# A two-layer gated cross-attention kernel: maxima subtracted on VectorE, three transposed low parts on GpSimd, all instruction streams in a new order

## The reference

```
x = x + tanh(g) * attention0(norm(x), ctx)    # 16 heads; softmax over the heads, not over the keys
x = x + tanh(g) * ffn0(norm(x))               # silu(x Wg) * (x Wu), hidden size 768, then Wd
x = x + tanh(g) * attention1(norm(x), ctx)    # 16 query heads, one shared key and value head
x = x + tanh(g) * ffn1(norm(x))               # one 256x256 matrix: W plus a low-rank product, and a bias
norm(x) = (x - mean(x)) / sqrt(var(x) + 1e-5)
```

## Time and profile before

| | |
|---|---|
| median of 3 runs | 2554.6 us (2552.17 to 2556.8) |
| the profiled execution | 2554.42 us |
| its span, first to last instruction | 2552.6 us |
| mean granted TensorE clock | 0.996 of full speed |
| busy: PE, DVE, ACT, POOL | 2463.6, 2311.4, 1616.7, 1476.5 us |

### The profile page before, as it was taken

The page is one execution under the profiler, slowest core; times in us unless marked ns, Lnnn a source line. Parts: engine busy times, 40 slices in busy tenths (PEclk is TensorE's granted clock), DMA queues, the critical chain, the costliest instruction groups (busy, mean ns, idle before and its releaser), DMA issues.

```text
span 2552.6 us, 70067 instructions
## 1 busy us (share of the span) xinstructions
PE 2463.6 (97%) x27972; PEld 2151.3 (84%) x27972; DVE 2311.4 (91%) x4254; ACT 1616.7 (63%) x3210; POOL 1476.5 (58%) x1806
## 2 busy tenths in 40 slices
PE   6999999999999999999999999999999999999997
PEld 5888888888888888888888888888888888888886
DVE  7889999999999999999999999999999999999974
ACT  4466666666666666666666666666666666666653
POOL 3555565565565565665665665665665665655642
PEclk9999999999999999999999999999999999999999
DMA  3000010010000010010110110110110100110100
GB/s 101 20 28 25 25 33 22 28 33 21 29 31 23 29 31 23 29 31 19 33 31 19 33 31 19 33 31 19 33 31 19 33 31 19 33 31 19 30 18 14
DMA packets 74322, 73.20 MB, mean 29 GB/s; under 512 B 6555, under 2 KB 73393, under 8 KB 74290
## 3 DMA queue, kind: packets, MB, share of 16 engines
q1 hardware_dynamic: 74290, 72.75, 9.2%
HBM read 54.90 MB, written 16.78 MB: 28 GB/s over the span
## 4 chain that ended last, share of the span: by engine, by line
PE 48%; DVE 46%; issue 3%; ACT 1%; POOL 0%; DMA 0%; SPq 0%; POOLq 0%; DVEq 0%; ACTq 0%
PE work L1849 11%; PE work L1850 9%; PE work L1851 9%; DVE m L1284 6%; DVE e L1302 6%; DVE m L1293 5%; PE scores L1952 5%; PE work L1985 5%; DVE x L1321 4%; DVE y_q L1312 3%; PE scores L1942 3%; DVE scores L1290 3%; PE work L1888 3%; PE work L1866 2%; DVE work L1298 2%
## 5 line engine op out<-in xcount | busy, mean ns | idle before, releaser
L731 ACT ACTIVATE e<-scores 120x1024 f32<-120x1024 f32 x512 | 497.4, 1023 | 133.2 <-PE scores L1952 97.0
L1849 PE MATMUL work<-xt_hi_B,w_hi 128*128 128x256 f32 x1536 | 452.4, 295 | 1.9 <-DVE xt_lo_B L1264 0.9
L1851 PE MATMUL work<-xt_hi_B,w_lo 128*128 128x256 f32 x1536 | 432.9, 282 | 0.0
L1850 PE MATMUL work<-xt_lo_B,w_hi 128*128 128x256 f32 x1536 | 432.8, 282 | 0.0
L388 POOL TENSOR_TENSOR h_lo<-h_f,h_hi 128x256 fp32r<-128x256 f32 x384 | 291.4, 772 | 219.7 <-ACT h_hi L681 219.7
L394 POOL TENSOR_TENSOR zt<-e 120x512 f32<-120x512 f32 x256 | 325.8, 1284 | 80.1 <-ACT e L731 80.1
L1849 PEld LDWEIGHTS work<-xt_hi_B,w_hi 128*128 128x128 f32 x1536 | 289.2, 188 | 58.4 <-issue 21.3
L1284 DVE TENSOR_REDUCE m<-scores 120x128 fp32r<-120x2048 f32 x128 | 291.7, 2279 | 3.1 <-PE scores L1942 3.1
L1302 DVE TENSOR_TENSOR e<-e,work 120x2048 f32<-120x2048 f32 x128 | 292.1, 2282 | 2.2
L681 ACT ACTIVATE h_hi<-h_f 128x256 fp32r<-128x256 f32 x384 | 157.1, 432 | 215.2 <-DVE h_f L1278 210.6
L1850 PEld LDWEIGHTS work<-xt_lo_B,w_hi 128*128 128x128 f32 x1536 | 289.5, 188 | 2.8
(11 more groups left out here) (213 smaller groups left out, 7299.1 us busy)
## 6 DMA issues: line engine op xcount, KB each, us to landing
x_res<-xp SPq DMA_DIRECT2D x64, 256.0 KB, 2.8
x_ln<-xp SPq DMA_DIRECT2D x64, 256.0 KB, 2.9
y<-y_out SPq DMA_DIRECT2D x64, 256.0 KB, 2.2
ctx_f_A<-cp SPq DMA_DIRECT2D x64, 128.0 KB, 2.1
ctx_f_C<-cp SPq DMA_DIRECT2D x64, 128.0 KB, 2.0
qm<-mT SPq DMA_DIRECT2D x256, 4.0 KB
e<-wi SPq DMA_DIRECT2D x3, 768.0 KB, 6.9
w_ctx<-wc SPq DMA_DIRECT2D x1, 656.0 KB
```

What stands on the lines that cost most here:

```text
L731: return act.activation(e[0:SC, c, 2 * h:2 * h + 2, :, :].rearrange("p a b n -> p (a b n)"), scores[0:SC, 2 * h:2 * h + 2, :].rearrange("p ...
L1849: pe.matmul(out, a_hi, b_hi_, start=first, stop=False, skip_group_check=parts)
L1850: pe.matmul(out, a_hi, b_lo_, start=False, stop=False, skip_group_check=parts)
L1851: last = pe.matmul(out, a_lo, b_hi_, start=False, stop=end, skip_group_check=parts)
```

## The change

VectorE now subtracts both halves of both maxima of attention 0, and the matmuls with the negative identity are gone. `transposed_lo` for B, C and D moves from VectorE to GpSimd. GpSimd can't read PSUM, so ScalarE first copies the transposed bank to a new SBUF tile `xt`, and then splits the high part from that tile. The negated mean and the variance plus eps, two small VectorE instructions per layer norm, become two small GpSimd instructions at the head of `root`. The lag grows from five to six, so the loop has 58 iterations, the prologue holds one more started batch, and the drain one more to finish. The core of the diff:

```diff
-DEPTH = 5
+DEPTH = 6
+        xt = {s: sb(f"xt_{s}", [P, KC, S]) for s in "BCD"}
             def root(st, t):
+                pool.tensor_tensor(var_eps[st][:, :], mv[st][:, :, 1], eps_tile[:, :], ALU.add).then_inc(s[f"ln_root_{st}"], 1)
+                pool.tensor_tensor(neg_mean[st][:, :], zero_tile[:, :], mv[st][:, :, 0], ALU.subtract)
+                pool.wait_ge(s[f"ln_root_{st}"], within(0, 2, t))
                 pool.tensor_tensor(rstd[st][:, :], var_eps[st][:, :], minus_half[:, :], ALU.pow)\
...
             def moments(st, x, t):
...
-                last.then_inc(s[f"ln_mom_{st}"], 1)
-                dve.wait_ge(s[f"ln_mom_{st}"], within(1, 2, t))
-                dve.tensor_scalar(neg_mean[st][:, :], mv[st][:, :, 0], -1.0, None, ALU.mult)
-                return dve.tensor_scalar(var_eps[st][:, :], mv[st][:, :, 1], EPS, None, ALU.add)
+                return last
...
+                act.activation(xt["B"][:, :, :], two(W[1], KC), ACT.Copy).then_inc(s["T_out_B"], 1)
+                act.wait_ge(s["T_out_B"], t)
+                split_hi(xt_hi["B"][:, :, :], xt["B"][:, :, :]).then_inc(s["T_hi_B"], 1)
...
+                pool.wait_ge(s["T_hi_B"], t)
+                pool.tensor_tensor(xt_lo["B"][:, :, :], xt["B"][:, :, :], xt_hi["B"][:, :, :].bitcast(F32), ALU.subtract)\
+                    .then_inc(s["T_lo_B"], 1)
...
+                subtract_max(1, 0).then_inc(s["A1_sub_dve"], 1)
+                subtract_max(1, 1).then_inc(s["A1_sub_dve"], 1)
```

More of the change, by code:

```diff
@@ L2032, in _ @@
+            transposes(W[3], "A").then_inc(s["T_mm_A"], 1)
             pe.wait_ge(s["T_lo_A"], 4)
[L2033 to L2040 removed]
@@ L2119, in _ @@
[L2119 to L2124 removed]
+            pe.wait_ge(s["ld_ctx_A"], 112)
+            pe.wait_ge(s["mT_out"], 7)
+            keys0(W[3]).then_inc(s["k0_mm"], 1)
+            pe.wait_ge(s["q_out_A"], 7)
+            rows_out(W[2], y_hi["A"], y_lo["A"], "wo0", False).then_inc(s["woA_mm"], 1)
@@ new lines, in _ @@
+            pe.wait_ge(s["max_rows"], 448)
+            pe.wait_ge(s["A1_exp"], 14)
+            scores1(0).then_inc(s["T0_mm"], 1)
+            pe.wait_ge(s["T0_exp"], 14)
+            scores1(1).then_inc(s["T1_mm"], 1)
+            pe.wait_ge(s["res_A"], 7)
+            attended1(W[2], 0).then_inc(s["yz0_mm"], 1)
+            pe.wait_ge(s["ln_B"], 7)
+            transposes(W[3], "B").then_inc(s["T_mm_B"], 1)
+            keep_busy(W[0], 2)
+            pe.wait_ge(s["T1_exp"], 14)
+            scores0(0).then_inc(s["A0_mm"], 1)
@@ new lines, in _ @@
+            pe.wait_ge(s["G_h"], 38)
+            attended0(W[1], 0).then_inc(s["yA0_mm"], 1)
+            attended0(W[1], 1).then_inc(s["yA1_mm"], 1)
+            pe.wait_ge(s["G_h"], 39)
+            pe.wait_ge(s["ld_ctx_C"], 96)
+            keys_values1(W[0]).then_inc(s["kv1_mm"], 1)
+            pe.wait_ge(s["G_h"], 40)
+            pe.wait_ge(s["ln_C"], 7)
+            transposes(W[2], "C").then_inc(s["T_mm_C"], 1)
+            pe.wait_ge(s["G_h"], 41)
+            gate_up(W[3], 5).then_inc(s["G_mm"], 1)
@@ new lines, in _ @@
+            down(W[2], 3).then_inc(s["dn_mm"], 1)
+            pe.wait_ge(s["T_lo_C"], LAST)
+            queries(W[3], "C", "q1", False).then_inc(s["q_mm_C"], 1)
+            pe.wait_ge(s["kz1_odd"], LAST + 1)
+            rows_out(W[0], y_hi["C"], y_lo["C"], "wo1", False).then_inc(s["woC_mm"], 1)
+            pe.wait_ge(s["q_out_C"], LAST + 1)
+            key_scores(0).then_inc(s["M0_mm"], 1)
+            down(W[2], 4).then_inc(s["dn_mm"], 1)
+            values0(W[3]).then_inc(s["v0_mm"], 1)
@@ new lines, in _ @@
+            pe.wait_ge(s["M0_max"], LAST + 1)
+            key_scores(1).then_inc(s["M1_mm"], 1)
+            rows_out(W[0], y_hi["A"], y_lo["A"], "wo0", False).then_inc(s["woA_mm"], 1)
+            pe.wait_ge(s["G_lo"], 6 * LAST + 1)
+            down(W[2], 5).then_inc(s["dn_mm"], 1)
+            pe.wait_ge(s["M1_max"], LAST + 1)
+            scores0(1).then_inc(s["A1_mm"], 1)
+            maxima_transposed(W[3]).then_inc(s["mT_mm"], 1)
+            pe.wait_ge(s["res_B"], LAST + 1)
+            queries(W[2], "A", "q0", False).then_inc(s["q_mm_A"], 1)
@@ new lines, in _ @@
+            keep_busy(W[0], 9)
+            pe.wait_ge(s["T0_exp"], 2 * LAST + 2)
+            scores1(1).then_inc(s["T1_mm"], 1)
+            pe.wait_ge(s["A0_p"], LAST + 1)
+            attended0(W[0], 0).then_inc(s["yA0_mm"], 1)
+            pe.wait_ge(s["kz0_odd"], LAST + 1)
+            attended1(W[1], 0).then_inc(s["yz0_mm"], 1)
+            pe.wait_ge(s["T1_exp"], 2 * LAST + 2)
+            scores0(0).then_inc(s["A0_mm"], 1)
+            pe.wait_ge(s["ln_B"], LAST + 1)
+            pe.wait_ge(s["yz0"], LAST + 1)
@@ new lines, in _ @@
+            pe.wait_ge(s["G_lo"], 6 * LAST + 6)
+            down(W[3], 4).then_inc(s["dn_mm"], 1)
+            pe.wait_ge(s["G_lo"], 6 * LAST + 7)
+            down(W[3], 5).then_inc(s["dn_mm"], 1)
+            scores1(1).then_inc(s["T1_mm"], 1)
+            pe.wait_ge(s["T_lo_D"], LAST + 2)
+            rows_out(W[1], xt_hi["D"], xt_lo["D"], "f1", False).then_inc(s["f1_mm"], 1)
+            pe.wait_ge(s["res_A"], LAST + 2)
+            attended1(W[2], 0).then_inc(s["yz0_mm"], 1)
+            attended0(W[3], 0).then_inc(s["yA0_mm"], 1)
```

2892 lines of the change are left out of this document (1578 added, 1314 removed), and 12 rows, old and new, of tables (given, passing).

## The result

The changed kernel takes 2444.55 us (median of 4 runs, 2444.3 to 2448.7), the kernel before 2554.62 beside it (2552.17 to 2556.8): a ratio of 0.9573, 95% interval 0.9557 to 0.959. I had said 2488, in a range of 2455 to 2548: the direction was right, the gain of 110 us is larger than the range allowed.

A forecast was written before the change was run, and what follows sets the result against it. TensorE and VectorE share the path, TensorE's floor being 36.80 us; with waits of 0.35 and 0.1 an iteration takes 37.25. 58 x 37.25 + 325 = 2485.5, plus 2 = 2488 us, range 2455 to 2548.

The forecast's parts named there:

- That is the floor: TensorE per iteration without idle or the removed matmuls: 38.48 - 0.74 - 0.94 = 36.80 us.
- the prediction's own walk: The new streams followed once around an iteration with start-to-start prices per block, to find where engines wait.
- The removed matmuls: TensorE's four matmuls with the negative identity: 0.47 us per pair, 0.94 us less per iteration.
- Wait (a): From the end of attended1(1) to the next iteration's transposes D: TensorE idles 0.25 to 0.8 us, 0.35 taken.
- (b): From the end of attended1(1) to rows_out C: TensorE has 5.4 us of work against 5.2, or 5.7 with slow `weigh`.
- (c): From scores0(1) to scores1(0): 6.3 us of TensorE work against 5.9 plus up to 0.4; 0.1 idle taken.
- The slack of xt_lo_B: Low part of B, now made on GpSimd, expected to arrive 0.4 us before `gate_up 0`.
- The port: VectorE's `weigh` sharing SBUF ports with GpSimd: expected 0.8 us, with GpSimd idle there, instead of 1.30.
- The rival's chance of 28%: First rival: `weigh` meets a GpSimd instruction, +0.54 us, iteration 37.8, time 2519 us; chance 28%.
- The floor rival: Hand-overs taken too large, TensorE's stream hardly idle: 36.85 us per iteration, 2464 us; chance 15%.
- Slower: Probability 0.13, mostly from a late GpSimd instruction on TensorE's path: 38.5 us per iteration, 2560 us, that rival 14%.
- Prologue and drain: Time outside the loop, now six batches' work: 281.7 + 43 = 325 us, expected between 313 and 337.

The follow-up runs named there:

- e5_back: Kernel after with the two new 8-byte tiles (eps, zero) allocated last, so activation operands move back by 64 bytes; 2455.04 us, ratio 0.9614.
- e4_half: Kernel after with the second subtraction of half 0 handling one bank of two, so it does not compute the reference; 2428.75 us, ratio 0.9509.
- e3_port: Kernel after with one more GpSimd subtraction of 128x512 per iteration, released to run beside `weigh`; 2507.66 us, ratio 0.9818.
- f4_alone_max: Kernel before, old order, with VectorE subtracting all four halves of the maxima in the loop and TensorE's four negative-identity matmuls gone; 2699.3 us, ratio 1.0571.
- e2_four: Kernel after with four added matmuls of 512 columns per iteration just ahead of transposes C; 2483.93 us, ratio 0.9724.
- e10_low: Kernel after with VectorE instead of GpSimd taking the low parts of C and D in the loop; 2483.17 us, ratio 0.9698.
- f3_late: Kernel after with GpSimd's last residual ahead of the low part of B instead of behind it in the loop; 2538.48 us, ratio 0.9938.

## Why the prediction was wrong where it was

**The step that failed** is "That is the floor": TensorE's 36.80. It measured 35.85, so all of the 0.94 us per iteration is in this term. The subtraction 38.48 - 0.74 - 0.94 took everything that the profile books as busy for work, at the old addresses and in the old order. Three things were in it. First, addresses: 0.36, shown by e5_back; in the period it is 0.16, about 10 us. The other two make up the 0.59 that remain at equal addresses (36.80 - 36.21).

Second, waits booked as busy. The loop before holds some 0.65 of them: 0.27 at rows_out D, 0.10 at transposes B, an estimated 0.2 before `gate_up 0`, and 0.07 before keys_values1, where the last matmul ahead of the 0.21 of idle is booked 0.07 longer than the last of the same block without a wait behind it. e5_back has some 0.34 left by the same reading: 0.07 before transposes D, 0.17 before `gate_up 0`, 0.10 at `gate_up 1` and scores1(0). So 0.3 of the 0.59 is waiting that went away. Third, order: one change to the 32-row and 32-column blocks less is 0.19. About 0.1 stays open. The addresses were tried by runs; the other two parts are read from the traces, and for the waits e4_half (+ 0.10 of busy without work), e3_port (+ 0.26) and f4_alone_max (0.70) bear it out. No run separates the order.

The prices of the prediction's own walk come out lower than the subtraction: 11 products at 1.44, 6 slices at 0.72, four score blocks at 1.2, keys0, values0 and four attended halves at 1.0, transposes 4 x 0.45 + 0.4, keys_values1 0.9, and scores1 2 x 1.1, for which the walk gives no price, make 36.3, next to the 36.21 of e5_back. I let the subtraction overrule them. That they meet so closely is luck in part, since the 36.21 still hold 0.34 of waiting.

**The removed matmuls** at 0.94: right (e2_four adds 1.04 of busy with four of that size, 0.10 of it waiting), but their worth depends on the rest of the change (f4_alone_max).

**VectorE** at 35.6, busy 34.5 to 35.5: high, it is busy 34.05, with 1.05 in front of head_max(1), as said. The sum 35.81 - 0.9 kept the 0.55 for which `weigh` stood behind GpSimd. **ScalarE** 27 and **GpSimd** 28.5: 26.66 and 27.63. The longer way of a low part is 1.23 by its own terms, not 1.3; nothing hangs on it.

**Wait (a)** 0.35 taken, 0.46 measured; at the old addresses 0.26. It does set the pace (e3_port, e4_half, e10_low). **(b)** and **(c)** are not seen by over 0.1. The slack of xt_lo_B was 0.4 in my walk and is none: `gate_up 0` starts as it ends, with some 0.15 of waiting booked as busy, and f3_late, where it is about 1.7 late, makes TensorE wait 1.61. That no idle time shows there hid a wait that I had not forecast.

**The port:** no collision, `weigh` 0.75, as walked, though h_lo 4 ends 0.6 us ahead of it and not a microsecond. The rival's chance of 28% was for the right mechanism at half its price.

**The floor rival** (15%, 2464) had the right direction and, for lack of a lower floor, the wrong size; the range ended at 2455 because I took 36.75 for the least that can be. **Slower** (13%) did not come, though f3_late shows that one instruction's place decides it.

**Prologue and drain** 325, measured 337, at the end of 313 to 337. Why the ends took 12 more than I chose, at the upper bound, was not tried; most of the growth lies in the drain.
